# Sixteen-head attention loop: the values product of four heads in one run, some copies moved to ScalarE, one batch's closing products spread

## The reference, cut to what matters

```python
Q, K, V = (proj(Wq, bq), proj(Wk, bk), proj(Wv, bv))          # 16 heads of 16
scores = jnp.einsum('bhqd,bhkd->bhqk', Q, K) * scale
dense_out = jnp.einsum('bhqk,bhkd->bhqd', jax.nn.softmax(scores + bias, axis=-1), V)
out = out.transpose(0, 2, 1, 3).reshape(Bb, Ss, Dd)
return out @ Wo.T + bo
```

## Time and profile before

| | us |
|---|---|
| median of three runs | 2113.58 |
| the profiled execution, its own time | 2099.86 |
| its span | 2098.1 |
| TensorE busy in the span | 1908.6 (91%) |
| VectorE busy | 1121.4 (53%) |
| ScalarE busy | 944.6 (45%) |
| first and last bias add of the loop start at | 840.8 and 1387.7 |

### The profile page before, as it was taken

One profiled execution on the slowest core, in us unless ns is written; L12 is line 12 of the kernel. 1 busy time (PEld: TensorE's weight loads), 2 busy tenths in 40 slices (PEclk: granted clock), 3 DMA queues, 4 the chain that ended last, 5 costly groups with the idle time before them and its releaser, 6 DMA issues.

```text
span 2098.1 us, 37599 instructions
## 1 busy us (share of the span) xinstructions
PE 1908.6 (91%) x15665; PEld 1372.2 (65%) x15665; DVE 1121.4 (53%) x2309; ACT 944.6 (45%) x1644; POOL 449.3 (21%) x502
## 2 busy tenths in 40 slices
PE   5888977995988949899999999999999999999998
PEld 3456965773656645667776776766777777777776
DVE  4474443016142126878887888854545543455544
ACT  2212022112242304778887888854454543445522
POOL 1352100004121033212121212112222222233313
PEclk8879567996998979999999999999999999999999
DMA  4000021112242339621100310000000000000001
GB/s 128 0 1 1 1 66 42 57 47 61 81 140 81 101 118 169 128 42 37 33 23 19 104 31 25 19 21 1 1 1 2 1 1 1 27 1 1 2 1 40
DMA packets 85194, 86.94 MB, mean 41 GB/s; under 512 B 34658, under 2 KB 70946, under 8 KB 84898
## 3 DMA queue, kind: packets, MB, share of 16 engines
q1 hardware_dynamic: 79154, 73.81, 13.2%
q0 software_dynamic: 3072, 8.39, 1.4%
q10 hardware_dynamic: 2800, 2.34, 0.4%
HBM read 65.65 MB, written 18.87 MB: 40 GB/s over the span
## 4 chain that ended last, share of the span: by engine, by line
PE 74%; DVE 18%; issue 3%; DMA 2%; POOL 1%; ACT 1%; SPq 0%; DVEq 0%; POOLq 0%
PE PS L1032 7%; DVE arena L1695 7%; PE PS L1024 7%; PE PS L1899 6%; PE PS L1883 6%; PE PS L1838 5%; PE PS L1528 5%; PE PS L1541 5%; PE PS L1873 5%; DVE arena L1700 4%; PE PS L519 3%; PE PS L1520 3%; PE PS L1843 3%; PE PS L1906 1%; PE PS L1933 1%
## 5 line engine op out<-in xcount | busy, mean ns | idle before, releaser
L1695 DVE CUSTOM_DVE_ANT_0 arena<-PS,arena 128x1024 f32<-128x1024 f32 x256 | 312.8, 1222 | 75.3 <-PE PS L1520 62.4
L1528 PE MATMUL PS<-arena 128*128 128x128 f32 x2048 | 281.8, 275 | 20.4 <-DVE arena L1700 20.2
L1619 ACT ACTIVATE arena<-arena 128x1024 f32<-128x1024 f32 x256 | 295.0, 1152 | 9.8 <-DVE arena L1695 9.8
L1528 PEld LDWEIGHTS PS<-arena 128*128 128x128 f32 x2048 | 241.4, 142 | 87.4 <-DVE arena L1700 34.8
L1980 ACT ACTIVATE arena<-arena 128x449 f32<-128x449 f32 (+1 forms) x256 | 162.5, 635 | 190.8 <-DVE arena L2014 190.8
L2069 POOL TENSOR_SCALAR arena<-arena 128x448 f32<-128x448 f32 (+1 forms) x256 | 154.3, 616 | 419.4 <-DVE arena L2005 419.4
L2014 DVE CUSTOM_DVE_ANT_0 arena<-PS,arena 128x448 f32<-128x448 f32 (+1 forms) x256 | 141.2, 590 | 138.9 <-PE PS L1874 138.0
L1615 ACT COPY arena<-PS 128x512 f32<-128x512 f32 x256 | 150.4, 588 | 102.9 <-PE PS L1528 94.7
L1700 DVE COPY arena<-PS 128x512 f32<-128x512 f32 x256 | 175.9, 687 | 1.2 <-PE PS L1528 1.2
L1024 PE MATMUL PS<-arena 128*128 128x512 f32 x384 | 170.2, 601 | 6.6 <-ACT arena L1123 6.6
L1032 PE MATMUL PS<-arena 128*128 128x256 f32 x768 | 172.2, 385 | 0.0
(11 more groups left out here) (279 smaller groups left out, 2657.0 us busy)
## 6 DMA issues: line engine op xcount, KB each, us to landing
arena<-in_L_ffn_W SPq DMA_DIRECT2D x16, 1024.0 KB, 6.6
arena<-prior SPq DMA_DIRECT2D x16, 512.0 KB, 4.0
parts<-arena SPq DMA_DIRECT2D x24, 256.0 KB, 5.4
arena<-parts SPq DMA_DIRECT2D x96, 64.0 KB, 2.9
arena<-parts SPq DMA_DIRECT2D x48, 128.0 KB, 10.5
ye<-arena SPq DMA_DIRECT2D x8, 512.0 KB, 3.5
prior<-arena SPq DMA_DIRECT2D x4, 1024.0 KB, 9.1
arena<-in_xT SPq DMA_DIRECT2D x2, 1024.0 KB, 8.0
```

The costliest lines, as they stand in the source:

```text
L1528: h = e.transpose(PS[:, i, P * j:P * j + P], Sb[z % 3][:, 512 * g + P * j:512 * g + P * j + P], ident)
L1619: e.activation(Sb[z % 3], Sb[z % 3], ACT.Exp, bias=mr[:, z % 4:z % 4 + 1], scale=-1.0).then_inc(s_exp, 1)
L1695: e.tensor_tensor_reduce(Sb[z % 3], ps, Ab[m % 2], 1.0, 3e38, ALU.add, ALU.min, mr[:, z % 4:z % 4 + 1]).then_inc(s_ttr, 1)
```

## The change

Three things are changed in `phase_e`:

1. The values of four heads are no longer in three pieces. All 32 products stand in one run, once in four steps, at step k+7 (k the first unit of the four), and on TensorE ahead of that step's turn, no longer behind it. The output copy on ScalarE comes in step k+7, no longer k+8.
2. For every sixth unit (k % 6 == 5; 42 units) ScalarE copies both halves of the turn, in order ahead of its exponential, and VectorE has no copy. Among four units whose values are summed together, the unit so treated is in turn the first turned behind the values run (k % 4 == 1) and the last but one (k % 4 == 3).
3. Batch 0's eight closing pieces stand at steps 135, 139, 143, 147 (transposes) and 155, 161, 167, 173 (matmuls), no longer at 135 to 142. Batch 1's stay.

```diff
@@ -1395,26 +1395,28 @@
         for c in range(2):
             w.wait_ge(s_fp[o][c], 48)
 
+
+    CLOSE = {135 + 4 * k if k < 4 else 131 + 6 * k: (0, k) for k in range(8)}
+    CLOSE.update({263 + k: (1, k) for k in range(8)})
+
     def closing(z):
-        for b in range(B):
-            k = z - 23 - 16 * (8 * b + 7)
-            if 0 <= k < 8:
-                return b, k
-        return None
+        return CLOSE.get(z)
+
+    def turned_by(z, g):
+
+        return "act" if g or z % 6 == 5 else "dve"
 
     def gathered(z):
         return (z - 23) // 16 if z >= 23 and (z - 23) % 16 == 0 and (z - 23) // 16 < NM else None
 
     def summed(z):
 
-        if z >= 5 and (z - 5) // 4 < NZ // 4 and (z - 5) % 4:
-            return (z - 5) // 4 * 4, ((0, 1, 2), (3, 4, 5), (6, 7))[(z - 5) % 4 - 1]
-        return None
+        return z - 7 if z >= 7 and (z - 7) % 4 == 0 and z - 7 < NZ else None
 
     for z in range(NZ + 15):
         if 2 <= z < NZ + 2:
-            ring.plan(("t", z - 2, 0), "dve")
-            ring.plan(("t", z - 2, 1), "act")
+            for g in range(2):
+                ring.plan(("t", z - 2, g), turned_by(z - 2, g))
         if gathered(z) is not None:
             ring.plan(("g", gathered(z)), "dve")
         if closing(z) is not None:
@@ -1528,19 +1530,19 @@
                     h = e.transpose(PS[:, i, P * j:P * j + P], Sb[z % 3][:, 512 * g + P * j:512 * g + P * j + P], ident)
                 h.then_inc(ring.sem, 1)
 
-        def values(z, ks):
+        def values(z):
             b, h, g = z // 16 // TB_, z % 16, z % 16 // 4
-            for x in range(2):
-                w.wait_ge(*ring.emptied(("t", z + 3, x)))
+            for d in range(4):
+                for x in range(2):
+                    w.wait_ge(*ring.emptied(("t", z + d, x)))
             w.wait_ge(s_ot, z // 4)
             w.wait_ge(*pring.emptied(("V", b, 3)))
             w.wait_ge(s_one, 2)
             w.wait_ge(s_oz, 1)
-            for k in ks:
+            for k in range(8):
                 for d in range(4):
                     i = e.matmul(PS[32 * d:32 * d + 17, OBK, P * g:P * g + P], V4[b][:, k, h + d, :], Pt[(z + d) % 8][:, P * k:P * k + P], start=k == 0, stop=k == 7)
-            if ks[-1] == 7:
-                i.then_inc(s_val, 1)
+            i.then_inc(s_val, 1)
 
         def gather(m):
             w.wait_ge(s_ot, 4 * m + 4)
@@ -1568,10 +1570,10 @@
         for z in range(NZ + 15):
             if z < NZ:
                 scores(z)
+            if summed(z) is not None:
+                values(summed(z))
             if 2 <= z < NZ + 2:
                 turn(z - 2)
-            if summed(z):
-                values(*summed(z))
             if gathered(z) is not None:
                 gather(gathered(z))
             if closing(z):
@@ -1610,21 +1612,22 @@
                 last = s if s[0] == "P" else None
 
         def turn(z):
-            key = ("t", z, 1)
             w.wait_ge(s_val, (z - 8) // 4 + 1)
-            e.copy(Pt[z % 8][:, 512:1024], PS[:, group(key), :]).then_inc(ring.into(key), 1)
+            for g in range(2):
+                if turned_by(z, g) == "act":
+                    key = ("t", z, g)
+                    e.copy(Pt[z % 8][:, 512 * g:512 * g + 512], PS[:, group(key), :]).then_inc(ring.into(key), 1)
 
         def expo(z):
             w.wait_ge(s_ttr, z + 1)
             e.activation(Sb[z % 3], Sb[z % 3], ACT.Exp, bias=mr[:, z % 4:z % 4 + 1], scale=-1.0).then_inc(s_exp, 1)
 
-        def values(z, ks):
-            if ks[-1] == 7:
-                g, m = z % 16 // 4, z // 16
-                w.wait_ge(s_val, z // 4 + 1)
-                if m:
-                    w.wait_ge(*ring.filled(("g", m - 1)))
-                e.copy(OT[:, P * g:P * g + P], PS[:, OBK, P * g:P * g + P]).then_inc(s_ot, 1)
+        def values(z):
+            g, m = z % 16 // 4, z // 16
+            w.wait_ge(s_val, z // 4 + 1)
+            if m:
+                w.wait_ge(*ring.filled(("g", m - 1)))
+            e.copy(OT[:, P * g:P * g + P], PS[:, OBK, P * g:P * g + P]).then_inc(s_ot, 1)
 
         def close(b, k):
             key = ("c", b, k)
@@ -1695,6 +1698,8 @@
             e.tensor_tensor_reduce(Sb[z % 3], ps, Ab[m % 2], 1.0, 3e38, ALU.add, ALU.min, mr[:, z % 4:z % 4 + 1]).then_inc(s_ttr, 1)
 
         def turn(z):
+            if turned_by(z, 0) != "dve":
+                return
             key = ("t", z, 0)
             w.wait_ge(s_val, (z - 8) // 4 + 1)
             e.tensor_copy(Pt[z % 8][:, 0:512], PS[:, group(key), :]).then_inc(ring.into(key), 1)
```

## The result

The changed kernel takes 2099.32 us (median of five runs, 2095.6 to 2101.65) against 2113.58 us before: ratio 0.9943, 95% interval 0.993 to 0.9957, so 12 us faster. That is a small change, but clear of the noise. Forecast was 2121 us and slower. Two later measurements of the same kernel gave 0.9931 (0.9908 to 0.9953) and 0.9952 (0.9936 to 0.9968). Its profiled execution has a span of 2094.6 us.

What follows compares the result with a forecast made beforehand. A cycle going through TensorE and VectorE by turns was taken to bound the loop. 7.4 + 0.5 - 0.5 + 0.3 = +7.7, rounded to +7.5, made 2107.4, and 13.7 more 2121 us; range 2104 to 2130 for 8 in 10.

Steps and rivals of the forecast that it cites:

- run of values: Four steps of the attention loop take 8.34 us against 8.22, 62 times: +7.4 us.
- 42 extra copies on ScalarE: ScalarE taking VectorE's copy of half 0 in the loop gains nothing: +0.5 us, ends 0 and +4.
- the walk: Start-to-start links followed through four steps of the new attention loop; their sum is 8.34 us against 8.22.
- output copy to A 0.39: ScalarE in the loop: 0.39 us from the output copy's start to its next copy of a turned half.
- A to E 0.53: ScalarE in the loop: 0.53 us from the start of its copy of a turned half to the exponential's.
- rival 3: ScalarE's chain in the loop becomes the last, slower still: +6 us on top, 2128; chance 0.10.
- Rival 2: No difference: four steps of the loop 8.15 to 8.25, -4 to +2 us, 2110 to 2116; chance 0.24.
- about two in four steps: How often TensorE's half turn waits on VectorE's copy in the loop, read from 127 waits, 55.1 us.
- rival 1: TensorE bounds the loop and the 0.34 us saved reaches the end: -21 us, 2093; chance 0.12.
- closing pieces: Spreading batch 0's closing products over steps 155 to 173: -0.5 us, ends -1 and +0.5.
- loop's end: The run at step 255 stands whole between last scores and last two turns: +0.3 us, 0 to +0.8.
- Rival 4: TensorE's stall amid batch 1's loads vanishes or recurs: 4 to 6 us either way; chance 0.04 of turning sign faster.

Runs made afterwards that it cites:

- e1_no_copies: The changed kernel with every half 0 copied by VectorE again, run of values and spread closing pieces kept; 1.0004 against the kernel before.
- e7: The kernel before (values in three pieces) with half 0 of units k % 4 == 3 copied by ScalarE; 0.9814 against the kernel before.
- e8: The kernel before with half 0 of units k % 4 == 3 copied by ScalarE and batch 0's closing pieces spread; 0.985 against the kernel before.
- e13: The kernel before with half 0 of units k % 4 == 3 copied by ScalarE and batch 1's keys loaded later; 0.9845 against the kernel before.
- e4_copies_k3: The changed kernel with ScalarE's extra copies for units k % 4 == 3 (64 copies), not every sixth; 0.9876 against the kernel before.
- r2_changed_third: The changed kernel, nothing altered, measured a third time; 0.9952 against the kernel before.
- e5_copies_k5of12: The changed kernel with only the 21 extra copies of units k % 12 == 5 on ScalarE; 1.0004 against the kernel before.

## Why the prediction was wrong

Two terms failed, and only together do they turn the sign: with the copies alone as measured the prediction's sum would be -1 us, with the run of values alone +1, with both -7.

The larger is the **42 extra copies on ScalarE**, taken as +0.5 us with ends 0 and +4. For the 21 behind the run it said gain 0, and they gained 0 (1.0004 without any, 1.0004 with these). For the other 21 it said "Gain 0" because the copy would come at 7.18 of the walk and the half turn at 7.85, the same as by VectorE. They came at 6.75 (1231.98, the scores being at 1225.23), and gained 0.35 to 0.43 in each of their groups, 21 x 0.4 = 8 us. The step in it that failed is the link "output copy to A 0.39", 0.25 of the 0.43 by which the copies came earlier. It was read off two starts, but A there waits for the transposes that start 1.07 ahead of it (1006.23 to 1007.30), the same distance as where the row names them:

```profile
1004.25 1.04 PE L1528 MATMUL PS<-arena 128*128 128x128 f32 x8
...
1005.32 0.59 ACT L1615 COPY arena<-PS 128x512 f32<-128x512 f32 x1 [0.52 <-PE PS L1528]
```

With its data ready A follows in 0.14. With that one link mended the prediction's walk gives a half turn at 7.60, a gain of 0.24 in each of the 21 groups. The link "A to E 0.53" has the same fault in small: E at 1007.83 is 1.27 behind its B, and with B done it follows A in 0.48. The rest is the chain's start, 0.07 earlier (3.54 for 3.61), and links 0.01 to 0.04 shorter. The kernel before had the warning in it: ScalarE stood idle ahead of 195 of its 256 copies A, on the transposes (us, times):

```profile
  PE PS L1528: 94.7, 195
```

A link that ends on a wait is not the engine's own pace. The same error made ScalarE's chain seem 0.08 from the end, on which rival 3 rested, where the doubled output copy showed room. And the lower end of the term was 0, though its edit takes a wait off the end of the cycle and all that held the gain at 0 was this one estimate of ScalarE's time.

The **run of values** was priced 0.09 too dear: 8.34 forecast, 8.25 measured. No single link was far off (0.54, 1.90, 0.97 forecast; 0.53, 1.88, 0.93 measured, and 0.02 over VectorE's links). Against the 8.22 or 8.23 of before the forecast was 62 x 0.12 = +7.4; measured is 62 x 0.02 = +1, and 0 by the timed runs. So the mechanism, that a long run starves VectorE and pays back what it saves, was right; the size was not. Rival 2 had the time of the cycle (8.15 to 8.25), but not by its mechanism: scores to values cost 0.53 and not 0.45. A difference of two sums of some nine links, each rounded to 0.01, is multiplied by 62 here, and the middle was stated as if it were better than its own bounds.

One reading of the prediction was wrong without harm to the sum: 127 waits are not "about two in four steps". The earlier trace rows counts weight loads (63) and matmuls (64) of the same stop, and the earlier trace rows shows it once in 8.22 us. So the argument against rival 1, that of two such waits in four steps one remains, does not hold as it stands: there was one, and it stayed (in e1_no_copies the matmuls stood for D 16.6 us in 76 times).

The **closing pieces**: -0.5 forecast. Steps 128 to 175 take 109.3 us in e1_no_copies against 109.8, while its twelve groups there are 0.02 longer each: -0.7. The **loop's end**: +0.3 forecast; from the last B to the end of the span are 711.5 to 712.5 us with the run of values, 710.4 to 711.3 before, 710.1 to 710.6 in most of the versions in pieces: about +1.2.

Rival 4, the stall, was real but was booked on the range; the profile of before happened to hold a long one.

Summed, 1 - 8 - 1 + 1 = -7 us by the steady groups, against -12, -15 and -10 measured. A part of the rest is the clock. Each execution has its own mean granted clock, and the phases ahead of the loop, the same in every version, differ by it. Their first 830 us in the second and third profile of the changed kernel, where the first B starts at 832.4 and 854.3 (columns as in the earlier trace rows):

```profile
0.00:830.00 830.00, 686.04 (x3637) 482.48 (x3637) 317.85 (x547) 197.29 (x304) 172.10 (x148) 0.86 0.24 69
```

```profile
0.00:830.00 830.00, 682.96 (x3572) 479.06 (x3573) 304.02 (x526) 186.17 (x286) 167.67 (x138) 0.83 0.22 66
```

Among the 98 executions of the kernel before that were timed beside the versions, a mean clock 0.001 higher goes with 1.7 us less (correlation -0.87). The executions of the second measurement of the changed kernel had 0.9360, those of the kernel before beside them 0.9324: some 6 of its 15 us. An estimate by this line puts the second and third measurement at 10 and 9 us, and e7, e8 and e13, whose loops are equal but whose ratios go from 0.9814 to 0.985, at 34, 34 and 36 us, each good to 2 us or so. For the first measurement the clocks of the kernel before are not on record. What is left between -7 and -9 or -10 is **not settled**; it may be a stall that is on average shorter in the changed kernel, but by profiles its length overlaps between the two.

## What to carry to other kernels

The cycle here, which alternates between engines, was shortened only where one of its last links went, and there by up to the whole wait and the restart (0.53 in pieces, 0.35 to 0.43 behind the long run, where other waits come next), while the same edit two units away was worth nothing: find which half tile waits, and move that one. A link between two starts is an engine's pace only if the second instruction had its inputs; otherwise it is an upper bound. When equal kernels differ by more than the change, look at the clock that each execution was granted. And before trusting a walk whose result is multiplied by the loop count, test it against a place where the edit removes a link, not only against the loop as it is.

## What the runs showed of the hardware

The stall of TensorE in its values came in all 15 profiles with the key loads in their first place (0.7 to 4.3 us). With the loads later it was gone from there in all four, and stood at the new place in two (1.3 and 2.7 us). The traces' DMA packets say what TensorE most likely waited for. Packets of 16 KB and of the kind "instruction" pass on queue q8 about every 9 us in this part of the loop; ahead of five of the stalls there is one gap of 20 to 22 us (874.57 to 894.89 in the kernel before), and in all 17 stalls TensorE went on 1.4 to 1.9 us after the end of such a packet (896.60, then 898.42). That these packets hold TensorE's instructions is inferred from this timing, not shown by itself.

What the stall drew after it differed. The kernel before, two stretches from the end of its 3.35 us (columns as in the earlier trace rows):

```profile
898.00:903.00 5.00, 4.58 (x40) 2.85 (x40) 1.84 (x3) 1.24 (x2) 0.00 (x0) 0.50 0.59 72
903.00:908.00 5.00, 4.93 (x46) 3.37 (x42) 3.49 (x6) 3.10 (x6) 0.00 (x0) 0.88 0.00 0
```

The granted clock is 0.50, the 1.2 GHz level, and then 0.88, both levels in turn. After 0.72, 0.79, 1.88 and even 2.98 us (e4_copies_k3) of standing it was 1.00 in the next ten; after 2.70 (r2_changed_third) 0.66 in the first five, after 3.12 (e5_copies_k5of12) 0.73. So where the clock falls, the stall's own length is a little over half its price (3.35 of the 6.2 us that the seventh group lost with it). A second unexpected number: ScalarE starts a 128 x 512 copy 0.14 us after the start of a 128 x 128 one that itself lasts 0.26, when the data are there.
